# Two cross-attention layers and an MLP: constant rows made by two engines, first stack transfers on two queues, the normalisation ahead of the tables, and layer 1's token blocks copied by VectorE

## The reference

```python
def layer0(ctx, x, mask, ...):          # x: (16, 256, 512), ctx: (16, 256, 512)
    h = concat([ctx, x], axis=1)        # 512 keys
    q = x @ q_w + q_b;  k, v = split(h @ kv_w + kv_b)
    a = softmax(where(mask, q k^T / 32, -inf))
    y = (a v) @ out_w + out_b + x
    y = y * rsqrt(mean(y*y) + 1e-6) * postnorm_w
    return gelu(y @ mlp_w1 + mlp_b1) @ mlp_w2 + mlp_b2 + x

def layer1(x, ctx, mask, ...):          # 256 keys
    n = (ctx - mean) * rsqrt(var + 1e-5) * gamma + beta
    q = x @ Wq.T;  k = n @ Wk.T;  v = n @ Wv.T
    a = softmax(where(mask, q k^T * 32**-0.5, -inf))
    return x + tanh(gate) * ((a v) @ Wo.T)

out = layer1(layer0(ctx, x, mask0, ...), ctx, mask1, ...)
```

## Time and profile before

| | |
|---|---|
| median of 3 runs | 2510.09 us (2508.76 to 2511.73) |
| the profiled execution's own time | 2504.85 us |
| its span in the profile | 2502.7 us |
| PE busy | 2371.9 us, 95% of the span |
| ACT busy | 1454.3 us, 58% |
| DVE busy | 1211.8 us, 48% |
| POOL busy | 232.1 us, 9% |
| layer 0, MLP, layer 1 begin at about | 0, 1077 and 1783 us |

### The profile page before, as it was taken

How to read it: one execution, slowest core, us unless ns; L and a number is a source line. 1 busy time by engine, 2 the same in 40 slices (tenths; PEclk the granted TensorE clock), 3 DMA queues, 4 the chain that set the end, 5 groups by cost and what they waited for, 6 DMA issues and landing times. The chain is left out here.

```text
span 2502.7 us, 43888 instructions
## 1 busy us (share of the span) xinstructions
PE 2371.9 (95%) x14656; PEld 1933.0 (77%) x14656; DVE 1211.8 (48%) x2382; ACT 1454.3 (58%) x3386; POOL 232.1 (9%) x260
## 2 busy tenths in 40 slices
PE   6999999999999999989999999999889999999998
PEld 5677777777777777668888888888678787777886
DVE  4455566566665666542122212211465666656564
ACT  3777777777777777743222222222277676767676
POOL 2000000000000000010000000000211212121210
PEclk9899999999999999889999999999899999999998
DMA  6244444444444443441011001102253535454443
GB/s 174 77 108 110 109 108 107 108 108 108 108 108 108 107 108 92 129 147 51 1 50 50 18 32 50 50 0 84 92 143 97 144 110 135 118 131 123 119 110 84
DMA packets 148186, 239.00 MB, mean 95 GB/s; under 512 B 25600, under 2 KB 59680, under 8 KB 148144
## 3 DMA queue, kind: packets, MB, share of 16 engines
q1 hardware_dynamic: 140944, 228.62, 33.8%
q10 hardware_dynamic: 7200, 9.84, 1.7%
HBM read 86.28 MB, written 25.21 MB: 45 GB/s over the span
## 5 line engine op out<-in xcount | busy, mean ns | idle before, releaser
L558 ACT ACTIVATE l_score_ps<-l_score_ps,l_neg_max 128x512 f32<-128x512 f32 (+1 forms) x1024 | 567.9, 565 | 186.9 <-DVE l_neg_max L787 186.9
L787 DVE TENSOR_REDUCE l_neg_max<-l_score_ps 128x1 f32<-128x512 f32 (+1 forms) x768 | 499.7, 685 | 81.2 <-PE l_score_ps L1069 77.7
L578 ACT ACTIVATE l_probs<-l_score_ps 128x1024 f32<-128x1024 f32 x384 | 382.2, 1017 | 80.2 <-PE l_score_ps L1102 78.1
L1434 ACT ACTIVATE mlp_hidden<-mlp_hidden_ps,mlp_b_col 128x512 f32<-128x512 f32 x128 | 88.3, 690 | 496.7 <-PE mlp_hidden_ps L67 496.7
L1069 PE MATMUL l_score_ps<-l_stack 97*128 97x512 f32 (+1 forms) x1024 | 315.1, 376 | 55.4 <-ACT l_score_ps L558 42.6
L1469 DVE TENSOR_TENSOR mlp_hidden_l<-mlp_hidden,mlp_hidden_h 128x512 fp32r<-128x512 f32 x128 | 92.4, 722 | 520.2 <-ACT mlp_hidden_h L1436 520.2
L1069 PEld LDWEIGHTS l_score_ps<-l_stack 97*128 97x128 f32 x1024 | 180.7, 200 | 106.0 <-ACT l_score_ps L558 77.7
L1102 PEld LDWEIGHTS l_score_ps<-l_stack 99*128 99x128 f32 x1536 | 213.2, 193 | 59.5 <-ACT l_score_ps L558 18.4
L1102 PE MATMUL l_score_ps<-l_stack 99*128 99x256 f32 x1536 | 244.8, 292 | 15.0 <-ACT l_score_ps L558 14.0
L558 ACT ACTIVATION_READ_ACCUMULATOR l_score_ps<-l_score_ps,l_neg_max 128x1 f32 x1024 | 223.0, 218 | 0.0
L65 PE MATMUL mlp_hidden_ps<-mlp_norm_h,mlp_w_l 128*128 128x512 f32 x512 | 200.5, 392 | 6.4 <-DVE mlp_norm_l L1464 6.4
(11 more groups left out here) (136 smaller groups left out, 4306.2 us busy)
## 6 DMA issues: line engine op xcount, KB each, us to landing
l_stack<-room SPq DMA_DIRECT2D x256, 192.0 KB
l_stack<-l_qk SPq DMA_DIRECT2D x196, 128.0 KB
l_stack<-room SPq DMA_DIRECT2D x128, 128.0 KB
l_stack<-l_qk SPq DMA_DIRECT2D x226, 64.0 KB
l_tokens<-in_x SPq DMA_DIRECT2D x16, 512.0 KB, 3.4
l_tokens<-in_ctx SPq DMA_DIRECT2D x16, 512.0 KB, 4.2
l_stack<-room SPq DMA_DIRECT2D x128, 64.0 KB
l_rows<-in_x SPq DMA_DIRECT2D x16, 512.0 KB, 3.3
```

Source lines behind the costliest of these rows:

```text
L558: m = act.activation(e, e, ACT.Exp, bias=neg_max[:, q, h:h + 1], accum_out=row_sum[:, q, h:h + 1])
L578: act.activation(probs[:, s % PROBS, :].rearrange("p (a b) -> p a b", a=2), score_ps[:, 2 * (s % 2):2 * (s % 2) + 2, :], ACT.Exp).then_inc ...
L787: dve.tensor_reduce(out, bank, AXIS_X, ALU.max, negate=True).then_inc(max_done, 1)
L1434: act.activation(hidden[:, m % HBUF, :], hidden_ps[m % 4][:, :], ACT.Gelu_apprx_tanh, bias=b1_col[:, m:m + 1])
```

## The change

Layer 0: POOL makes the two small constants and then the zeroed tiles and selects, and fills the constant rows of heads 8 to 15 before it waits for the vectors; DVE fills those of heads 0 to 7 as its first instruction. SP doesn't wait for the tokens ahead of the first weight loads. Of the first stack transfers, those of row groups 2 and 3 of both halves are issued by ACT, behind the last high part and ahead of the last split.

Layer 1: POOL makes the two small constants, normalises batch 0 and only then makes the tables and the constant rows; it waits for the vectors where it first needs them. DVE's `layer_norm(0)` stands ahead of split 3 and no longer ahead of split 2. ACT issues the transfers of row groups 2 and 3 of the first half, behind the high parts of items 5 and 6. DVE's `vectors_ready` moves behind the low part of the last item.

Layer 1, all batches: the high parts of the token blocks are made by DVE (`token_high`), directly ahead of their low parts, and no longer by ACT. A slot's first maximum comes behind them, and V's copies ahead of the first maximum of slot 5. One step moves from slot 3 to slot 1.

SP now waits for `ones_made` in place of `const_made`.

```diff
@@ -121,7 +121,7 @@
     AHEAD = RING if first else 0
 
     STEPS_AT_FIRST = [0, 0, 4, 4, 4, 4, 4, 4, 4, 4] if first else [0, 0, 2, 3, 3, 3, 3, 2]
-    STEPS_IN_SLOT = [2, 4, 4, 2, 1, 2, 1, 4, 4, 4] if first else [2, 0, 2, 2, 2, 3, 3, 2]
+    STEPS_IN_SLOT = [2, 4, 4, 2, 1, 2, 1, 4, 4, 4] if first else [2, 1, 2, 1, 2, 3, 3, 2]
     AFTER_T = SLOT.index(("item", NT))
     V_AHEAD = 1 if first else 2
     TURN_SLOT = AFTER_T
@@ -199,7 +199,7 @@
         o_ps = [pb(f"o_ps{n}", [P, D]) for n in range(2)]
 
 
-        ident_made, const_made = sem("ident_made"), sem("const_made")
+        ident_made, const_made, ones_made = sem("ident_made"), sem("const_made"), sem("ones_made")
         raw_loaded = [sem(f"raw_loaded{n}") for n in range(2)]
         w_turned, w_high, w_low = sem("w_turned"), sem("w_high"), sem("w_low")
         vec_loaded, mask_loaded, mask_made, mask_stored = (
@@ -305,7 +305,8 @@
             return [(gamma[:, :], vectors["gamma"].partition_broadcast(P)), (beta[:, :], vectors["beta"].partition_broadcast(P)),
                     (gate[:, :], vectors["gate"].partition_broadcast(P))]
         VECTORS = 5 if first else 3
-        CONSTS = 7
+        CONSTS = 6
+        ONES = 2 if first else 1
 
         def load_tokens(sp, b):
             sp.dma_start(tokens[:, 0:QT, :], x_view[b]).then_inc(tokens_loaded, 16)
@@ -337,9 +338,11 @@
 
         SLOTS_OF_ACT = {} if first else {HG - 2: (1, 2), HG - 1: (0, 1, 2)}
 
-        def every_slot(half, j):
-
-            return tuple(range(SPLIT))
+        FIRST_OF_ACT = [(HG - 2, HG - 1), (HG - 2, HG - 1) if first else ()]
+
+        def first_slots_of_sp(half, j):
+
+            return () if j in FIRST_OF_ACT[half] else tuple(range(SPLIT))
 
         def slots_of_sp(half, j):
 
@@ -357,7 +360,6 @@
             if first:
 
                 load_tokens(sp, 0)
-                sp.wait_ge(tokens_loaded, 32)
                 load_raw(0)
                 load_raw(1)
             with nc.allow_non_contiguous_dma(reason="per-feature vectors, once"):
@@ -375,7 +377,7 @@
             sp.wait_ge(mask_made, 1)
             sp.dma_start(mask_rows, mask_tile).then_inc(mask_stored, 16)
             sp.wait_ge(mask_stored, 16)
-            sp.wait_ge(const_made, CONSTS)
+            sp.wait_ge(ones_made, ONES)
 
             def iteration(p, a, prev):
                 def load_rows():
@@ -417,7 +419,7 @@
                             sp.wait_ge(shifted_done, PSTEPS * a + PSTEPS // HALVES * (half + 1))
                         load_stacks(sp, p, half, ITEMS * p + NT + NK + half + 1 if first
                                     else ITEMS * p + NT + GROUPS * (half + 1),
-                                    every_slot if a is None else slots_of_sp)
+                                    first_slots_of_sp if a is None else slots_of_sp)
                 if a is not None and not first:
                     sp.wait_ge(rows_done, a + 1)
                     sp.dma_start(out_view[a], rows[:, :, :]).then_inc(stored, 16)
@@ -441,18 +443,22 @@
             if first:
                 make_identity(pool, ident, ident_made)
                 pool.wait_ge(ident_made, 2)
-            pool.memset(f32(shiftT[:, :, :]), 0.0).then_inc(const_made, 1)
-            pool.memset(f32(spread[:, :, :]), 0.0).then_inc(const_made, 1)
-            for n, row in enumerate((INV_ROW, INV_LOW_ROW)):
-                pool.wait_ge(const_made, n + 2)
+            pool.memset(half_power[:, :], -0.5).then_inc(const_made, 1)
+            pool.memset(eps[:, :], RMS_EPS if first else LN_EPS).then_inc(const_made, 1)
+
+            def make_spread():
+                pool.memset(f32(shiftT[:, :, :]), 0.0).then_inc(const_made, 1)
+                pool.memset(f32(spread[:, :, :]), 0.0).then_inc(const_made, 1)
+                spread_rows()
+
+            def spread_rows():
                 by_head = spread[:, :, :].rearrange("p g (j d) -> p g j d", j=HG)
-                pool.affine_select(out=by_head, in_=f32(by_head), compare_op=ALU.not_equal, fill=1.0, base=-row,
-                                   pattern=[[-HG, GROUPS], [-1, HG], [0, DH]], channel_multiplier=1
-                                   ).then_inc(const_made, 1)
-            pool.wait_ge(const_made, 4)
-            pool.memset(half_power[:, :], -0.5).then_inc(const_made, 1)
-            pool.wait_ge(const_made, 5)
-            pool.memset(eps[:, :], RMS_EPS if first else LN_EPS).then_inc(const_made, 1)
+                for n, row in enumerate((INV_ROW, INV_LOW_ROW)):
+                    pool.wait_ge(const_made, n + 4)
+                    pool.affine_select(out=by_head, in_=f32(by_head), compare_op=ALU.not_equal, fill=1.0, base=-row,
+                                       pattern=[[-HG, GROUPS], [-1, HG], [0, DH]], channel_multiplier=1
+                                       ).then_inc(const_made, 1)
+
             def ln_rstd(b):
                 pool.wait_ge(stats_done, b + 1)
                 for t in range(QT):
@@ -463,6 +469,8 @@
                 n.then_inc(ln_rstd_done, 1)
 
                 pool.wait_ge(ln_step, 2 * (b + 1))
+                if isinstance(b, int) and b == 0:
+                    pool.wait_ge(vec_loaded, 16 * VECTORS)
                 for t in range(QT):
                     n = pool.tensor_tensor(tokens[:, QT + t, :], tokens[:, QT + t, :], gamma[:, :], ALU.mult)
                 n.then_inc(ln_scaled, 1)
@@ -488,14 +496,19 @@
                 if not first and p is not None and not (isinstance(p, int) and p == B - 1):
                     ln_rstd(p + 1)
 
-            pool.wait_ge(const_made, CONSTS - 1)
-            pool.wait_ge(vec_loaded, 16 * VECTORS)
-            if not first:
+            if first:
+                make_spread()
+                pool.wait_ge(const_made, CONSTS)
+                pool.memset(f32(stack[MASK_ROW:ROWS_ALL, HALF:HEADS, :]), 1.0).then_inc(ones_made, 1)
+                pool.wait_ge(vec_loaded, 16 * VECTORS)
+            else:
+                pool.wait_ge(const_made, 2)
                 ln_rstd(0)
                 pool.wait_ge(ln_done, 1)
-
-            pool.memset(f32(stack[MASK_ROW:ROWS_ALL, :, :]), 1.0).then_inc(const_made, 1)
-            pool.wait_ge(const_made, CONSTS)
+                make_spread()
+                pool.wait_ge(const_made, CONSTS)
+                pool.memset(f32(stack[MASK_ROW:ROWS_ALL, :, :]), 1.0).then_inc(ones_made, 1)
+            pool.wait_ge(ones_made, ONES)
             iteration(0, None)
             with pool.Fori(1, B - 1) as i:
                 iteration(i, i - 1)
@@ -527,7 +540,7 @@
                 ps, done = item_ps[k % 2], ITEMS * b + k + 1
                 if k < NT:
 
-                    if not isinstance(b, int) or b > 0:
+                    if first and (not isinstance(b, int) or b > 0):
                         if k < FB - 1:
                             act.wait_ge(v_shared, (FB - 1) * (b - 1) + k + 1)
                         else:
@@ -658,7 +671,7 @@
                         high(p, n)
 
                     kind, n = kind_of(slot, p, a)
-                    if kind == "item" and n < NT:
+                    if first and kind == "item" and n < NT:
                         high(p, n)
                     if a is not None:
                         if TURN_SLOT == slot - 1:
@@ -686,10 +699,18 @@
             for kind, n in FIRST:
                 if kind == "split":
                     split_high(n)
-                else:
+                elif first or n >= NT:
                     if n == NT:
                         vectors_ready()
                     high(0, n)
+                    if first and n == ITEMS - 1:
+                        for half in range(HALVES):
+                            act.wait_ge(low_done, NT + NK + half + 1)
+                            for j in FIRST_OF_ACT[half]:
+                                move_stack(act, half, j, range(SPLIT))
+                    if not first and n in (NT + 1, NT + 2):
+                        act.wait_ge(low_done, NT + GROUPS)
+                        move_stack(act, 0, FIRST_OF_ACT[0][n - NT - 1], range(SPLIT))
             iteration(1, 0)
             with act.Fori(2, B) as i:
                 iteration(i, i - 1)
@@ -753,6 +774,16 @@
                     n = dve.tensor_scalar(tokens[:, QT + t, :], tokens[:, QT + t, :], stat[:, t, 0:1],
                                           stat[:, t, 2:3], ALU.subtract, ALU.mult)
                 n.then_inc(ln_step, 1)
+
+            def token_high(b, k):
+
+                dve.wait_ge(item_done, ITEMS * b + k + 1)
+                if not isinstance(b, int) or b > 0:
+                    if k < FB - 1:
+                        dve.wait_ge(v_shared, (FB - 1) * (b - 1) + k + 1)
+                    else:
+                        dve.wait_ge(v_done, KB * b)
+                dve.tensor_copy(hT[0][:, k, :], item_ps[k % 2][:, :]).then_inc(high_done, 1)
 
             def low(b, k):
 
@@ -868,10 +899,19 @@
                 for slot in range(SLOTS + 1):
```

(26 more changed lines are left out.)

## The result

| | before | after |
|---|---|---|
| median of the runs | 2509.80 us (2508.76 to 2511.73, 4 runs) | 2485.15 us (2483.39 to 2487.28, 4 runs) |
| the profiled execution, its span | 2504.85, 2502.7 us | 2487.28, 2485.5 us |
| layer 1 begins at | 1783.5 us | 1780.9 us |

The ratio is 0.9904, 95% interval 0.9889 to 0.9919: 24.7 us less, where 15.9 were forecast (2494.2, range 2484 to 2507). The two profiled executions differ by 17.6 us only.

What follows compares the result with a forecast made beforehand. The prediction took PE to bound layer 1's iterations except in the first pass up to step 9, where ACT and then VectorE were late. Its terms, -5.3 + 3.2 - 12.6 - 1.2 = -15.9 us, gave 2494.2, range 2484 to 2507.

Steps and rivals of the forecast that it cites:

- Iterations, -12.6: Layer 1's 14 steady iterations: step 9 comes earlier, 0.9 us gained in each (bounds 0.3 and 1.1), 12.6 in all.
- Pairs of 1.32: Layer 1's iterations: a token block's high and low part, both on VectorE, cost 1.32 us together.
- 12.64: Layer 1's iterations, first pass: VectorE's summed work up to step 9, in us, starting step 9 1.1 us earlier.
- Rivals 2, 4 and 5: Whole kernel: half a gain, 2502.6 (chance 0.18); no change, 2506.8 or 2514 (0.08); VectorE the slower bound, 2521 (0.06).
- Rival 3: Whole kernel: the full 1.1 us in 14 iterations and a neutral layer 1 start, -23, so 2487; chance 0.08.
- the strict reading of full durations: Layer 1's iterations: all 17 large VectorE instructions cost 0.69 us, the sum is some 1.2 longer, the gain nil.
- Layer 0, -5.3: Layer 0's prologue: earlier constants and loads, less the second transfer queue's cost, gain 5.3 us (bounds -7 and +2).
- Layer 1's start, +3.2: Layer 1's prologue and iteration 1 up to step 9: 3.2 us lost in sum (bounds -1 and +7).
- the second low part: Layer 1's prologue, projection blocks: ends near 1806.9 where it was done by 1808.97 before.
- Drain, -1.2: Drain iteration: V is copied while VectorE idles, 1.2 us saved (bounds 0.8 and 1.3).
- The sum, -15.9: Whole kernel: -5.3 + 3.2 - 12.6 - 1.2 us, median 2494.2; as forecast has chance 0.60.

Runs made afterwards that it cites:

- `v_behind`: The changed kernel with V's two copies back behind the shift table in layer 1's iterations: 2501.5 us.
- `l0_stack_sp`: The changed kernel with layer 0's first stack transfers issued by SP alone, as before the change: 2482.0 us.
- `l1_start_undone`: The changed kernel with layer 1's prologue as before the change, VectorE still making batch 0's token blocks: 2481.5 us.

## Why the prediction was right, and where it was not

**Iterations, -12.6: right in sign, price and period, half wrong in cause.** Pairs of 1.32, 12.57 against 12.64, 1.16 an iteration against 1.1 (0.9 taken). Measured are -17.7: 2.9 of the difference by the 0.9, 2.2 by fewer stalls, a term that the forecast did not have. The clock, for which I took off 0.2, stayed high: PE's projection products began at 2166.24, ahead of the last block's low part. The step that failed is "ACT now needs only 8 x 0.9 = 7.2 us for steps 0 to 7 and is never late". In the changed kernel nothing contradicts it, since V's copies stand ahead of the table; with them behind it (`v_behind`) ACT is late although it has no token blocks. A sum of busy times leaves out that ACT follows three maxima made at 0.60 each with 0.9 each, so the table waits 0.80 for the last sum. The row that I quoted, the table's 1.48 idle before it, held the answer: V's copies fit there whoever copies the tokens. I used that for the drain and not for the iterations. Rivals 2, 4 and 5 are out: 1.32 a pair, 0.60 for a further copy. Rival 3 was nearest in time (2487), by the 14 x 1.1 and not by a neutral start; its own terms add up to -21.9, which is 2488, and not to -23. In the strict reading of full durations 15 starts, and not 17, were priced at 0.60, which makes 1.35 and not 1.2; its verdict stays the same.

**Layer 0, -5.3: right.** The mask row (0.22 for under 0.5), the first transfer at 32.7 for 33.1, ACT's transfers through at 47.4 (45.6 to 47.5), the first maximum at 52.21 (50.4 to 52.3) behind the output weights' low part, block 0 5.5 earlier, and 5.1 at the start of layer 1 over ten executions. That the second queue costs more than it buys is shown by `l0_stack_sp`.

**Layer 1's start, +3.2: right in kind, too small by 1.7 up to step 9 and by 2.7 with the rest of iteration 1,** which lacks 1.0 of the gain (42.12 for a period of 41.17; before, 42.26 for 42.33). The mis-sized step is the second low part, forecast 2.1 sooner (1806.9 for 1808.97): it ends 24.8 from the layer's start against 25.5, so 0.7 sooner. The tokens did come 2.5 sooner (first high part at 11.8 against 14.2) and PE began the projections 2.3 sooner, but the first block's products took 4.66 us at clock 0.63 and not 3.14 at 1.00. PE had idled 4.02 ahead of the token blocks' transposes (2.56 before); the executions above tie the low clock to the token blocks on VectorE. The forecast had weighed a low clock for the iterations and the V products, not here.

And ACT's eight transfers took 4.21 + 2.80 = 7.0 and not 5.4; one of them, at 1807.74, took 2.25, while SP's at 1808.03 took 1.96. Both push the last low part, which ends at 33.4 and not at 30.8, and so the scan. The V products then follow the split after 4.1 and not 3.0. From the V products' start to step 9 it is 16.8, as forecast, but by luck: the items listed for VectorE add up to 12.64 at their own prices and not to 13.8; it took 13.04, and what stood ahead of it 3.76 and not 3.0.

**Drain, -1.2: right**, 1.8 with what follows.

**The sum, -15.9, for -17.2 in the spans: partly luck.** The four parts missed by +2.7 (in this pair; not over ten executions), +1.7, -5.1 and -0.6, and most of that cancels.

**The gain of the medians, 24.7, is 8.8 above the 15.9.** 1.7 of it is in the two profiles (17.6 against 15.9). For the other 7.1: the profiled execution of before lies 5.0 under its median, that of after 2.1 above its own. The latter has the long end of layer 0, which leaves 1.1 to 1.2 at the start of layer 1. I had added the 5 us to the forecast unchanged; that they are mostly stalls, which the change makes shorter, I argue from the excess column, but unprofiled runs don't show their stages, so it stays open.

## What to carry to other kernels

Where an engine waits for another's answer, put there work of its own that is due soon: moving two copies of 0.6 us ahead of such a wait was worth the whole 1.2 us, while moving four copies between engines was worth nothing to the period. Add up each engine's work, but also follow the last handoff: an engine with less work than the bound can still be late at the one place that matters. Before moving something long off the path, list what stands behind its new place; the scan of 5.2 us cost more at the splits than it had cost ahead of the first low part.

## What the runs showed of the hardware

- In layer 0 transfers issued by SP and ACT at the same time cost each queue more: 0.85 each where SP alone took 0.67. In layer 1 that is not so: beside each other the two queues took 0.6 to 0.9 a transfer but for one of each, 2.25 on ACT's and 1.96 on SP's.
- The issue of a small transfer sometimes takes 1.2 to 2.0 us in place of 0.6, once or twice in layer 1's iterations of every traced kernel, on either queue, and can reach PE.
- The clock at the end of layer 0 falls one of two ways (10.1 or 12.1 us for 68 products), in executions of kernels that are alike there. In the iterations it was 0.92 to 1.00 before and is 1.00 now, but that was not the gain: before, iterations at 0.94 and at 1.00 both take 42.3, and in `v_behind` they take 42.15 at 1.00.
- The first projection block of layer 1 took 3.14 us at clock 1.00 where ACT makes the token blocks ahead of it and 4.4 to 5.4 at 0.52 to 0.67 where VectorE does. PE's idle ahead of the transposes doesn't explain it: 2.56 in the kernel before and in `l1_start_undone` (5.42 us at 0.52).
- A VectorE instruction of 0.22 us took 8.2 to 8.4 begun inside a fill by GpSimd, but a fill by VectorE beside one by GpSimd cost neither anything.
- A copy from PSUM rounded to the fast format costs VectorE 0.60 in a row of instructions, as a maximum or a subtraction does.
